# Second attention of a two-layer kernel: row maxima four steps late in a turn instead of two, and split maxima sent to the stacks within SBUF

## The reference, cut to what matters

```
q = (x @ Wq.T + bq).reshape(b, n, G, hpg, HD)     # 16 heads of 16, in G = 4 groups of hpg = 4
k = (x @ Wk.T + bk).reshape(b, n, G, HD)
v = (x @ Wv.T + bv).reshape(b, n, G, HD)
scores = einsum('bqghd,bkgd->bghqk', q, k) * scale
attn = softmax(scores, axis=-1)
y = einsum('bghqk,bkgd->bqghd', attn, v)
return y @ Wo.T + bo
```

## Time and profile before

| | |
|---|---|
| median of 3 runs | 802.94 us (802.45 to 804.71) |
| profiled execution, its own time | 802.42 us |
| span of the profiled execution | 800.6 us |
| TensorE busy | 734.7 us (92%) |
| VectorE busy | 578.3 us (72%) |
| ScalarE busy | 337.7 us (42%) |
| GpSimd busy | 133.0 us (17%) |

### The profile page before, as it was taken

How to read it: one execution, slowest core, us unless ns; L and a number is a source line. 1 busy time by engine, 2 the same in 40 slices (tenths; PEclk the granted TensorE clock), 3 DMA queues, 4 the chain that set the end, 5 groups by cost and what they waited for, 6 DMA issues and landing times.

```text
span 800.6 us, 14071 instructions
## 1 busy us (share of the span) xinstructions
PE 734.7 (92%) x4989; PEld 602.5 (75%) x4989; DVE 578.3 (72%) x1227; ACT 337.7 (42%) x597; POOL 133.0 (17%) x123
## 2 busy tenths in 40 slices
PE   3369995999999999899999999999999999999997
PEld 3259993799999999775444444444668999999997
DVE  6986767597777777857666666657785967777776
ACT  1215553533333333214777676665434333333332
POOL 0206652000000000071031542222530000000000
PEclk9999998999999999999999999999999999999999
DMA  8500000000000000074355654301400000000000
GB/s 328 214 1 1 0 1 0 1 1 1 1 0 0 0 0 0 2 184 96 74 105 78 120 111 96 48 17 27 185 1 1 1 1 21 1 20 20 20 20 20
DMA packets 21317, 36.38 MB, mean 45 GB/s; under 512 B 6316, under 2 KB 16972, under 8 KB 20504
## 3 DMA queue, kind: packets, MB, share of 16 engines
q1 hardware_dynamic: 16472, 33.12, 15.6%
q10 hardware_dynamic: 4800, 2.66, 2.0%
HBM read 25.79 MB, written 9.95 MB: 45 GB/s over the span
## 4 chain that ended last, share of the span: by engine, by line
PE 83%; DVE 10%; issue 2%; ACT 2%; DMA 1%; POOL 1%; DVEq 0%; SPq 0%; POOLq 0%
PE PS L1280 18%; PE PS L1282 17%; PE PS L1281 17%; PE PS L1546 7%; PE PS L1521 5%; PE PS L1530 5%; PE PS L1554 3%; PE PS L1637 2%; DVE MX L1192 1%; PE PS L1288 1%; PE PS L1363 1%; PE PS L1308 1%; DMA x_in<-in_x 1%; DVE stats L874 1%; PE PS L1397 1%
## 5 line engine op out<-in xcount | busy, mean ns | idle before, releaser
L1100 DVE SCALAR_TENSOR_TENSOR h<-PS,cmb,h 128x256 f32 (+1 forms) x342 | 144.5, 479 | 11.2 <-PE PS L1282 4.5
L1192 DVE TENSOR_REDUCE MX<-PS 128x2 f32<-128x576 f32 x144 | 108.6, 756 | 58.8 <-PE PS L1530 57.8
L698 ACT ACTIVATE PR<-PS 96x768 f32<-96x768 f32 x144 | 115.8, 807 | 55.8 <-PE PS L1521 55.2
L637 ACT ACTIVATE sg<-PS 128x384 f32<-128x384 f32 x114 | 55.9, 490 | 144.6 <-PE PS L1282 144.5
L1080 DVE TENSOR_TENSOR aa<-sg,PS 128x384 f32<-128x384 f32 x114 | 63.2, 554 | 74.2 <-ACT sg L637 73.9
L641 ACT ACTIVATE ah<-aa 128x384 fp32r<-128x384 f32 x114 | 60.0, 527 | 91.4 <-DVE aa L1080 91.4
L1280 PE MATMUL PS<-xTh,W1h 128*128 (+1 forms) x240 | 80.9, 337 | 0.0
L1282 PE MATMUL PS<-xTl,W1h 128*128 (+1 forms) x240 | 80.4, 335 | 0.0
L1281 PE MATMUL PS<-xTh,W1l 128*128 (+1 forms) x240 | 80.3, 335 | 0.0
L1280 PE MATMUL PS<-xTh,W0h 128*128 (+1 forms) x216 | 72.7, 337 | 0.2 <-DVE aa L1080 0.2
L1282 PE MATMUL PS<-xTl,W0h 128*128 (+1 forms) x216 | 72.4, 335 | 0.0
(11 more groups left out here) (240 smaller groups left out, 1568.5 us busy)
## 6 DMA issues: line engine op xcount, KB each, us to landing
QS<-scrH SPq DMA_DIRECT2D x28, 144.0 KB, 4.3
W1raw<-in_w SPq DMA_DIRECT2D x2, 1920.0 KB, 9.9
W0raw<-in_w SPq DMA_DIRECT2D x1, 3456.0 KB, 11.3
scrH<-qh SPq DMA_DIRECT2D x8, 432.0 KB, 2.4
scrL<-ql SPq DMA_DIRECT2D x8, 432.0 KB, 2.6
wD<-in_wD SPq DMA_DIRECT2D x1, 2304.0 KB, 11.8
out_tokens<-h SPq DMA_DIRECT2D x6, 384.0 KB, 2.3
x_in<-in_x SPq DMA_DIRECT2D x2, 1024.0 KB, 6.3
```

The source lines that it names most:

```text
L698: A_(PR[0:KT, ca:cb + 1:cb - ca, :], PS[0:KT, b:b + 2, 0:CW], ACT.Exp).then_inc(s["e_exp"], 1)
L1100: ins = V.scalar_tensor_tensor(out=hj, in0=PS[:, b + t // 2, (t % 2) * D:(t % 2) * D + D], scalar=cmb[:, ds(g * GT + t, 1), e:e + 1].squee ...
L1192: V.tensor_reduce(MX[:, hf, z:z + NSH // 2 + 1:NSH // 2], PS[:, b:b + 2, 0:POS], AX_X, ALU.max).then_inc(s["e_mx"], 1)
```

## The change

The transposes of maxima move from steps 11 and 3 to steps 13 and 5, and row scores start in step 4 of a turn instead of step 2, so four chunks of an image are done in the next turn instead of two. The functions `busy_at` and `late_busy` read `MT_U`, so filler moves too: step 12 of turn 1 gets one more, and turn 9 starts filler after step 5 instead of 3. In turn 1 the steps ahead of the first row scores hold ten fillers instead of six. The way through DRAM goes: four transfers per half, each nine rows of `Mh` or `Ml` into one row of `QS`, and `e_min0` and `e_min1` count to 64 per image. VectorE's wait before it overwrites `Mh` is now for the arrival of the same half of the image before.

```diff
-    scrM = nc.dram_tensor("scrM", (IMGS, 2, NS, P), F32, kind="Internal").ap()
...
-        def max_out(i, b):
+        def maxima_in(i, b):
 
             sp.wait_ge(s["e_msplit"], 2 * i + b + 1)
-            for n, src in enumerate((Mh, Ml)):
-                sp.dma_start(scrM[i, n, b * NSH:(b + 1) * NSH], src[:, b].bitcast(F32)).then_inc(s["e_mout"], 16)
-
-        def max_in(i, b):
-
-            sp.wait_ge(s["e_mout"], 32 * (2 * i + b + 1))
             for a in range(2):
-                r, c = TILE * a + MROW, b * NSH + a * (NSH // 2)
-                sp.dma_start(QS[i % NQB][r:r + 2, b * HQ:(b + 1) * HQ].bitcast(F32),
-                             scrM[i, :, c:c + NSH // 2].rearrange("n c r -> n (c r)")).then_inc(s[f"e_min{b}"], 16)
+                for n, src in enumerate((Mh, Ml)):
+                    r, c = TILE * a + MROW + n, a * (NSH // 2)
+                    sp.dma_start(QS[i % NQB][r:r + 1, b * HQ:(b + 1) * HQ].bitcast(F32).rearrange("p (c r) -> p c r", r=P),
+                                 src[c:c + NSH // 2, b].bitcast(F32)).then_inc(s[f"e_min{b}"], 16)
...
             if live(it, 2):
-                max_out(it - 2, 1)
-                max_in(it - 2, 1)
+                maxima_in(it - 2, 1)
             if live(it, 0) and it > 1:
                 for a in range(2):
                     stack_in(sp, it, a)
             if live(it, 1):
-                max_out(it - 1, 0)
-                max_in(it - 1, 0)
+                maxima_in(it - 1, 0)
...
-                    wait(dve, s["e_mout"], 32 * (2 * i + b - 1))
+                    wait(dve, s[f"e_min{b}"], 64 * i)
...
-                        pe.wait_ge(s["e_min0"], 32 * (i + 1))
+                        pe.wait_ge(s["e_min0"], 64 * (i + 1))
...
-                        pe.wait_ge(s["e_min1"], 32 * (i + 1))
+                        pe.wait_ge(s["e_min1"], 64 * (i + 1))
...
-MT_U = [11, 3]
+MT_U = [13, 5]
...
-S_LEAD = -2
+S_LEAD = -4
```

More of the change, by code:

```diff
@@ L290, in build @@
         e_const e_a1h e_a1 e_bo
-        e_pr e_prev e_split e_oh e_ol e_q0 e_in0 e_in1 e_in2 e_in3 e_vt e_va e_s e_mx e_mT e_msplit e_mout e_min0 e_min1
+        e_pr e_prev e_split e_oh e_ol e_q0 e_in0 e_in1 e_in2 e_in3 e_vt e_va e_s e_mx e_mT e_msplit  e_min0 e_min1
         e_st e_exp e_avt e_yr e_so e_sums e_ro e_rb e_rec e_y e_yt e_sb e_yl e_hi3
```

## The result

The changed kernel takes 822.7 us (median of 4 executions, 818.35 to 832.99) against 802.7 us (4 executions, 801.95 to 804.71) of the kernel before: a ratio of 1.023, 95% interval 1.021 to 1.025. The forecast was 802.2 us, range 799.8 to 805.0. The profiled execution of the changed kernel is its shortest: 818.35 us, span 816.6, so the profile must explain 16.0 us of span.

What follows compares the result with a forecast made beforehand. TensorE was taken as the bound (83% of the chain, transfers 1%). Terms of -0.8, +1.5, -1.4, -0.5 and +0.5 summed to -0.7 us, from 802.42 to 801.7, or 802.2 as median; range 799.8 to 805.0.

Steps and rivals of the forecast that it cites:

- four issues of about 0.3 us: SP's queue, per half of the maxima: old DRAM way and new SBUF-to-SBUF way both take four issues of about 0.3 us.
- Cost 0 in both places: Scores of step 9 and of the next turn: maxima land 1.0 and 1.3 us early, so transfers cost nothing.
- Rival B: Step 9: the half sent at step 5 lands over 2.5 us after its last issue, stalling scores; 805 to 808; chance 0.15.
- TensorE's clock is full throughout the stage: Second attention: the granted clock stays full, and five fillers less in all do not leave TensorE idle.
- The sum of the moves, -0.7 us: Whole change: -0.8 in turn 1, +1.5, -1.4 and -0.5 in the middle turns, +0.5 in turn 9.
- +1.5, -1.4 and -0.5: Middle turns: transpose exposed in step 5, +1.5 us; seven waits for `Ml` gone, -1.4; first row scores hidden in step 4, -0.5.
- T in step 5: Transpose of maxima moved from step 3: exposed there, +0.26 us in each of turns 3 to 8.
- The projections' waits: Turns 2 to 8: seven waits for `Ml`, five of a projection and two of filler, go; -1.4 us.
- Turn 9's filler: End of step 6: filler due at 542.0 waits for `Ml` until 543.5, so turn 9 gives +0.5 us, not -1.0.
- Rival A: The sum as forecast, with errors of 0.05 us per turn and a filler or two: 801 to 803.5; chance 0.6.
- C: Losses don't come: the step 5 transpose hides or turn 9's filler doesn't wait; 800.7, with both 799.2; chance 0.17.
- D: No effect on the ends: turn 2's start hangs on image 0's split, losing the 0.8; 803.0; chance 0.08.

Runs made afterwards that it cites:

- the probes: Changed kernel plus 27 small probe transfers on SP's queue, nine forms three times; kernel time not compared; median issue 0.52 to 0.71 us within SBUF, 0.22 to 0.27 with DRAM.
- the kernel with old steps: Changed kernel with its four SBUF-to-SBUF transfers kept but transposes back in steps 11 and 3, row scores from step 2: 803.97 us, ratio 1.003.
- run 2: Changed kernel, maxima transfers replaced by constants written before the first stacks: new steps 812.72 us; plus step 3 filler 817.77; only transposes moved 816.58; old steps 814.44.
- run 8: Changed kernel with two transfers per half instead of four, same data: new steps 802.17 us; plus two fillers ending step 3 in turns 3 to 8 800.65; old steps 803.37.
- run 3: Changed kernel, maxima transfers replaced by constants written behind the stacks of images 0 and 1: new steps 802.6 us; plus step 3 filler 801.46; old steps 802.59.
- run 7: Changed kernel without the transfers of `Ml` (rows hold -1), so two issues per half instead of four: 803.59 us, ratio 1.001.

## Why the prediction was wrong, point by point

- **The step that failed**: "Both cost SP four issues of about 0.3 us", and with it "Cost 0 in both places". The 0.3 came from rows with DRAM at one end; within SBUF an issue takes 0.70 to 0.75 (the same in the probes and in the kernel with old steps). That is 1.4 us of the 1.7 by which the way is longer than forecast; the hop itself, 1.83 for 1.47, gives 0.36. Against a spare of 1.0 and 1.3 us that makes a wait at 15 of 16 halves, 12.9 us. The prediction let the hop vary, not the issues. Rival B's own mechanism, a landing more than 2.5 us after the last issue, came once (2.99 us in turn 5) and nearly once more (2.45 in turn 8); in most halves the hop was 1.83 to 1.97, and the spare was used up before the last issue went out. So B named the symptom, for a mostly different reason.
- The 2.0 us that the prediction took from the Trainium skill (DMA: Bandwidth & Descriptors, Anatomy of one DMA) and weighed against 1.47 was the nearer figure for the hop (1.83), though that section describes transfers issued through GpSimd. It would not have changed the forecast, since most of the missing time was in the queue.
- **"TensorE's clock is full throughout the stage"** failed too. True of the kernel before in this stage, it isn't of one that waits: 0.60 in 367 to 384 us, and by the estimates above 9 us or more of the median's 20. The range had no case in which the clock falls. Three of the kernels of run 2 show the same behind another wait.
- Old way and spare: the prediction costed the new way alone. The kernel before, given the new steps, loses 18.6 us between the medians (2.1% by the ratio). By the probes its way takes 3.45 us, as much as the prediction's own times leave at step 5 (`Ml` at 423.95, scores at 427.4), so any longer hop is a wait.
- **The sum of the moves, -0.7 us, has the right sign and was too small.** Between medians at high clock it is -0.6 without transfers and -1.0 with two issues. The profiles tell the parts: turns 2 to 8 take 164.96 us together with two issues and filler, 165.86 before, -0.9 where +1.5, -1.4 and -0.5 gave -0.4; from turn 9 on +0.4, forecast +0.5. Turn 1: the first scores come 15.78 us after the first filler with two issues (351.13 to 366.91), 16.89 before, -1.1, forecast -0.8; but the kernel of run 8 with the old steps, whose turn 1 is the old one, has 16.61, so this is known to 0.3 us only. T in step 5: 0.26, as forecast. The projections' waits: gone, as forecast. The idling of step 4: 0.78 where 0.5 was forecast, the same in all kernels without filler there. Turn 9's filler: 0.97 of waiting for `Ml`, forecast 1.5, on the mechanism named.
- Rival A's condition, no wait for the maxima, was met only with the transfers gone, halved or paired (runs 3, 7 and 8); C and D didn't come.

**What stays open.** Why an issue within SBUF takes longer wasn't tried further than the six forms, nor why single hops took 2.45 and 2.99 us. And when the clock falls: all four executions of the changed kernel are at 0.973 or less, but a single fall can't be put down to a single wait. The idling of 0.77 us in step 4 stood within 1.6 us ahead of a fall in the profiles of three kernels (runs 2, 3 and 8), and is there in turns without any. The profiled execution of run 7, the longest of its 13 (811.61 us), falls at 371 us like the changed kernel and stays low to about 398, with no wait for maxima and 0.40 us of idling ahead, as much as the kernel before has there without a fall:

```profile
368.10 0.42 PE L1518 MATMUL PS<-QS,KS 50*96 50x384 f32 x2 [0.40 <-DVE MX L1189]
...
371.16 1.01 PE L1551 MATMUL PS<-xTh 128*128 128x384 f32 x2
```

Executions below 0.985 were 5 of 12 without the filler and 3 of 12 with it (run 3), 3 and 1 of 12 (run 8), 3 of 12 with the old steps, and 8 of 29 of the kernel before on that chip. That the filler of step 3 protects the clock is therefore argued, not shown. That the kernel with it is faster than the kernel before is shown (800.65 against 802.81 us at high clock); which part of that the filler brings is not.

## What to carry to other kernels

Before a transfer's route is changed, count its issues on the queue as well as its hops, and take their length from a row with the same two ends: a queue issues one after the other, and four issues of 0.7 us outweighed the hop that was saved. A step move that shortens a producer's lead should be checked against the whole way from the last write to the landing, for the old route too. And a wait of TensorE has two prices. In turns at full clock 1.2 us of new waits cost 0.7, since other waits shrink; but slower matmuls can follow it, and in the execution with 12.9 us of these waits the time grew by 16.0, in the median by 20.

## What the runs showed of the hardware that was not expected

- SP's queue takes 0.50 to 0.71 us to issue a small transfer from SBUF to SBUF (one row or 128), and 0.22 to 0.27 us with DRAM at one end (medians by form).
- A small transfer with its wait, on a quiet queue: 1.25 us into DRAM, 1.6 out of it, 1.65 to 1.9 within SBUF. In the pipeline, from its issue to its landing, the hop within SBUF took 1.83 us in most halves and up to 2.99.
- In three of four kernels a wait of 1.8 to 3.0 us at the start of turn 1 was followed by TensorE at half clock for 20 to 45 us in the profiled execution. The four took 10 to 15 us longer than the kernel before; with the wait removed, three of them ran at 801.5 to 802.6.
- Across the 29 executions of one kernel the time grew by 0.57 us for each 0.001 of mean granted clock.
